# Flamingo-style decoder stack on Trainium2: in the first layer's prelude, ScalarE instead of VectorE takes the first block of each transposed pair out of PSUM

## The reference, cut to what matters

```python
def _rmsnorm(x, weight):
    var = jnp.mean(jnp.square(x), axis=-1, keepdims=True)
    return x * jax.lax.rsqrt(var + EPS) * weight
x = _rmsnorm(hidden_states, ln_weight)
h_q = (x @ w_q.T).reshape(b, lq, H, DH)
h_k = (key_value_states @ w_k.T).reshape(b, lk, H, DH)
h_v = (key_value_states @ w_v.T).reshape(b, lk, H, DH)
```

## Time and profile before

| | |
|---|---|
| median of 3 runs | 1596.53 us (1595.96 to 1597.42) |
| the profiled execution | 1596.18 us |
| its span in the trace | 1594.5 us |
| TensorE matmul, busy | 1556.7 us, 98% |
| TensorE weight load | 1278.7 us, 80% |
| VectorE | 984.2 us, 62% |
| ScalarE | 796.1 us, 50% |
| POOL | 484.2 us, 30% |
| mean granted TensorE clock | 0.999 |

### The profile page before, as it was taken

How to read it: one execution, slowest core, us unless ns; L and a number is a source line. 1 busy time by engine, 2 the same in 40 slices (tenths; PEclk the granted TensorE clock), 3 DMA queues, 4 the chain that set the end, 5 groups by cost and what they waited for, 6 DMA issues and landing times.

```text
span 1594.5 us, 26459 instructions
## 1 busy us (share of the span) xinstructions
PE 1556.7 (98%) x9066; PEld 1278.7 (80%) x9066; DVE 984.2 (62%) x2597; ACT 796.1 (50%) x2279; POOL 484.2 (30%) x350
## 2 busy tenths in 40 slices
PE   9999999999999999999999999999999999999987
PEld 7788888888888888888886888888898788766556
DVE  6762663635636446265476676767676767756677
ACT  5442443434424344244342476667677332288874
POOL 3131320312203213032112613232323543377651
PEclk9999999999999999999999999999999999999999
DMA  5110111101111111111234011020202613000001
GB/s 182 54 44 30 57 43 53 43 30 56 43 39 43 43 56 43 39 43 44 67 93 159 14 40 53 20 72 0 79 1 80 226 54 105 17 11 14 5 2 53
DMA packets 36597, 85.67 MB, mean 54 GB/s; under 512 B 5808, under 2 KB 18736, under 8 KB 34480
## 3 DMA queue, kind: packets, MB, share of 16 engines
q1 hardware_dynamic: 36528, 84.80, 16.2%
HBM read 82.69 MB, written 2.10 MB: 53 GB/s over the span
## 4 chain that ended last, share of the span: by engine, by line
PE 78%; DVE 9%; ACT 4%; issue 3%; DVEq 2%; POOL 1%; DMA 1%; POOLq 0%; SPq 0%; ACTq 0%
PE banks L1288 10%; PE banks L1233 10%; PE banks L1206 10%; PE banks L1214 10%; PE banks L1448 9%; PE banks L1561 4%; PE banks L1345 3%; PE banks L1328 3%; PE banks L1526 3%; PE banks L1335 2%; PE banks L1668 2%; PE banks L1675 1%; PE banks L1691 1%; PE banks L1474 1%; PE banks L1698 1%
## 5 line engine op out<-in xcount | busy, mean ns | idle before, releaser
L559 POOL TENSOR_TENSOR w_q<-w_raw_q,w_q 128x1792 fp32r<-128x1792 f32 x15 | 61.1, 4071 | 479.3 <-ACT w_q L796 479.3
L1288 PE MATMUL banks<-w_o,atT 128*128 128x512 f32 x720 | 181.0, 396 | 0.0
L1206 PE MATMUL banks<-cT,w_k 128*128 128x512 f32 x720 | 178.0, 396 | 0.0
L1233 PE MATMUL banks<-w_v,cT 128*128 128x512 f32 x768 | 176.6, 390 | 0.0
L1233 PEld LDWEIGHTS banks<-w_v,cT 128*128 128x128 f32 x768 | 143.9, 188 | 29.8
L1214 PE MATMUL banks<-xT,w_q 128*128 128x512 f32 x672 | 163.7, 394 | 0.7 <-ACT kT L786 0.7
L2004 DVE TENSOR_TENSOR sA<-banks,pbias 128x512 f32<-128x512 f32 x62 | 42.7, 690 | 186.6 <-PE banks L1328 185.8
L1206 PEld LDWEIGHTS banks<-cT,w_k 128*128 128x128 f32 x720 | 131.9, 188 | 25.5
L1288 PEld LDWEIGHTS banks<-w_o,atT 128*128 128x128 f32 x720 | 131.7, 188 | 25.6
L1214 PEld LDWEIGHTS banks<-xT,w_q 128*128 128x128 f32 x672 | 123.7, 188 | 26.1 <-ACT kT L786 1.2
L855 ACT ACTIVATE sA<-sA,nmA 128x128 f32<-128x128 f32 x248 | 96.4, 393 | 55.8 <-DVE nmA L2009 55.5
(11 more groups left out here) (298 smaller groups left out, 3403.4 us busy)
## 6 DMA issues: line engine op xcount, KB each, us to landing
wo_raw<-in_wo SPq DMA_DIRECT2D x16, 768.0 KB, 4.4
w_raw_v<-in_w0v SPq DMA_DIRECT2D x8, 1024.0 KB, 4.7
w_raw_q<-in_w0q SPq DMA_DIRECT2D x16, 512.0 KB, 3.3
w_raw_k<-in_w0k SPq DMA_DIRECT2D x15, 512.0 KB, 3.4
w_raw_o<-in_w0o SPq DMA_DIRECT2D x15, 512.0 KB, 3.3
cTp<-in_ctxT SPq DMA_DIRECT2D x12, 512.0 KB, 4.3
wq_raw<-in_wq SPq DMA_DIRECT2D x1, 3072.0 KB, 10.2
x_res<-in_x SPq DMA_DIRECT2D x4, 512.0 KB, 11.4
```

The costliest lines, as they stand in the source:

```text
L559: pool.tensor_tensor(w_part[slot][1][:], w_raw[slot][:], w_part[slot][0][:].bitcast(F32), ALU.subtract).then_inc(S(f"w{slot}_lo"), 1)
L1206: mm = pe.matmul(dst, wk_[l][:, c, h * P:(h + 1) * P], cT[r][:, c, half * HT:(half + 1) * HT], start=c == 0 and n == 0, stop=c == DC - 1 a ...
L1233: mm = pe.matmul(dst, cT[l][:, c, b * P:(b + 1) * P], wv_[r][:, c, :], start=n == 0, stop=n == 3 * DC - 1)
L1288: mm = pe.matmul(dst, at_at(l, p, b // 4 * 2 + h)[:, t], w[r][:, h, :], start=start and n == 0, stop=stop and n == 5)
```

## The change

ScalarE gets a new step, `rows_scale(k)`: four activation copies of 128x128 out of bank 4, each with one column of the norm's weight as its scale, into the half of `stage[k]` that VectorE filled before. It stands ahead of the value stores of blocks 2 to 5, ahead of `rows_high(k)`; the one of pair 3 waits for the first `x_split`, since it writes the buffer of pair 0. VectorE's `rows_sums(k)` now multiplies bank 5 alone and then waits for ScalarE's block (`xl_ready`) before the differences. TensorE's `turn_x` waits for `xl_ready` for bank 4 and for `xw_ready` for bank 5. On VectorE `rows_sums(2)` moves ahead of Q's low part, and `rows_sums(3)` ahead of `rows_low(1)`. ScalarE's wait for the small loads (`g_loaded`) moves ahead of the loop. What is computed stays the same.

```diff
             def rows_high(k):
                 t = slice(k * P, (k + 1) * P)
                 if k == NPAIR - 1:
-                    act.wait_ge(S("xw_ready"), 3 * k + 2)
+                    act.wait_ge(S("xw_ready"), 2 * k + 1)
                     act.activation(xT[0][:, 0:2, :, t], stage[k][:, 0:2], ACT.Copy).then_inc(S("x_prep"), 1)
-                    act.wait_ge(S("xw_ready"), 3 * k + 3)
+                    act.wait_ge(S("xw_ready"), 2 * k + 2)
                     act.activation(xT[0][:, 2:, :, t], stage[k][:, 2:], ACT.Copy).then_inc(S("x_prep"), 1)
                     return
-                act.wait_ge(S("xw_ready"), 3 * k + 3)
+                act.wait_ge(S("xw_ready"), 2 * k + 2)
                 act.activation(xT[0][:, :, :, t], stage[k][:], ACT.Copy).then_inc(S("x_prep"), 1)
+
+            def rows_scale(k):
+                act.wait_ge(S("xr_used"), 2 * k + 1)
+                for c in range(DC):
+                    e = act.activation(stage[k][:, 2 + c // 2, c % 2, :], bank(4)[:, c * P:(c + 1) * P], ACT.Copy,
+                                       scale=ln_w[:, c:c + 1])
+                e.then_inc(S("xl_ready"), 1)
...
+            act.wait_ge(S("g_loaded"), 64)
             for b in range(2, NB):
+                if b < 2 + NPAIR:
+                    if b == 2 + NPAIR - 1:
+                        act.wait_ge(S("x_split"), 1)
+                    rows_scale(b - 2)
                 store_v(b, bank(b % 2), K_UNITS + b + 1)
                 if b < 2 + NPAIR:
                     rows_high(b - 2)
                 if b == 2:
                     round_q(0)
-            act.wait_ge(S("g_loaded"), 64)
             act.activation(gates[:], gates[:], ACT.Tanh).then_inc(S("gates_ready"), 1)
...
                     pe.wait_ge(S("xr_ready"), 2 * k + j + 1)
-                    if k > 0:
-                        pe.wait_ge(S("xw_ready"), 3 * (k - 1) + j + 1)
+                    if k > 0 and j == 0:
+                        pe.wait_ge(S("xl_ready"), k)
+                    if k > 0 and j == 1:
+                        pe.wait_ge(S("xw_ready"), 2 * k - 1)
...
             def rows_sums(k):
                 x = stage[k]
-                for j in range(2):
-                    dve.wait_ge(S("xr_used"), 2 * k + j + 1)
-                    dve.tensor_tensor(x[:, 2 - 2 * j:4 - 2 * j].rearrange("p s c t -> p (s c) t"),
-                                      bank(4 + j).rearrange("p (c t) -> p c t", c=DC),
-                                      ln_w[:].unsqueeze(2).to_broadcast([P, DC, P]), ALU.mult).then_inc(S("xw_ready"), 1)
+                dve.wait_ge(S("xr_used"), 2 * k + 2)
+                dve.tensor_tensor(x[:, 0:2].rearrange("p s c t -> p (s c) t"), bank(5).rearrange("p (c t) -> p c t", c=DC),
+                                  ln_w[:].unsqueeze(2).to_broadcast([P, DC, P]), ALU.mult).then_inc(S("xw_ready"), 1)
+                dve.wait_ge(S("xl_ready"), k + 1)
                 dve.drain()
...
             rows_sums(1)
             rows_low(0)
+            rows_sums(2)
             dve.wait_ge(S("wq_hi"), 1)
             dve.tensor_tensor(w_part["q"][1][:], w_raw["q"][:], w_part["q"][0][:].bitcast(F32),
                               ALU.subtract).then_inc(S("wq_lo"), 1)
-            rows_sums(2)
+            rows_sums(3)
             rows_low(1)
-            rows_sums(3)
             rows_low(2)
```

## The result

The changed kernel takes 1600.32 us (median of 12 runs, 1598.85 to 1601.89), the kernel before 1596.24 us (12 runs, 1594.25 to 1597.76): ratio 1.0024, 95% interval 1.0015 to 1.0033, so slower: the medians are 4.1 us apart, and the interval reaches from 2.4 to 5.3 us. Measured again beside other kernels it gave 1.0026 (1.0016 to 1.0036). The forecast was 1600.8.

A forecast was written before the change was run, and what follows sets the result against it. TensorE, busy 98% of the span, bounds the kernel, with VectorE second in the prelude. +3.00 and +1.74 us, less late savings, give +4.30 at query unit 0: 1600.8 us, range 1598.5 to 1603.1.

The forecast's parts named there:

- The two causes: ScalarE's prelude order: first block behind the diagonals, +3.00 us; second behind round_q, +1.74 us more by pair 1.
- nothing behind query unit 0 gives the delay back: After the prelude: TensorE's work is a chain of products in unchanged order, so the +4.30 us stays whole.
- VectorE as the second bound: In the prelude: VectorE has no idle time from 26.65 to 52.19; its last split leaves query unit 0 0.2 us slack.
- A: In the prelude: ScalarE's order makes new TensorE waits, query unit 0 4.30 us later; 1600.8 us; chance 0.55.
- B: In TensorE's new 3.75 us wait before turn_x(2): clock falls, at most +3.2, taken as 1.7 us; 1602.5; chance 0.20.
- C: On ScalarE: scaled copies out of PSUM cost no more than plain ones; +2.6 us, 1599.1 us; chance 0.12.
- D: On ScalarE: scales start when their bank is full, the 2.15 us gap goes; 2.4 us gained, 1594.1; chance 0.10.

The follow-up runs named there:

- second trace of the changed kernel: The changed kernel run again with no edit, beside other kernels on one chip: 1599.90 us, ratio 1.0026.
- dve_order: The kernel before with only VectorE's new order (the change's last hunk), ScalarE doing nothing new: 1595.97 us, ratio 1.0002.
- filler_two: The changed kernel with idle TensorE products in both new waits, 5 after value unit 2 and 13 after unit 3: 1600.76 us, ratio 1.0028.
- act_order: The changed kernel with three of ScalarE's four scaled blocks, and the small-loads wait, moved in its program order: 1593.92 us, again 1595.16 us.
- first_only: The changed kernel with only the first scaled block moved, behind value store 1, ahead of the last four diagonals: 1596.00 us, ratio 1.0004.
- act_part: The changed kernel with VectorE's order of before, so ScalarE's copies alone: 1600.36 us, ratio 1.0031.
- the last two kernels: act_order and the changed kernel, each with VectorE's mask step moved from ahead of the query sums to among them: 1593.63 and 1599.58 us.

## Why the prediction was right, point by point

**Right, as forecast.** The three `turn_x` starts were forecast at 31.08, 39.37 and 44.17. The first two came at 31.04 and 39.60; the third came at 47.11, with the clock lost. In the second trace of the changed kernel, whose first statistics are 0.58 us earlier than in the kernel before, the last two stand at 38.87 and 43.49, that is 39.45 and 44.07 on the forecast's scale. The two causes (the first block behind POOL's power and the diagonals, the second behind `round_q`) were each shown by moving one block. That nothing behind query unit 0 gives the delay back was right to 0.4 us up to POOL's L600, once the collision of the mask step is set apart; the rest of the span varies by 3.2 us. VectorE as the second bound, with 0.2 us of slack, was right: `dve_order` gained nothing.

**The sum.** A's +4.30 us at query unit 0 was +3.94 with the clock kept (37.80 - 33.86). Four copies took 1.12 us and not 1.28: 362 ns each, against 386 for the diagonals, whose source lies in SBUF, and 277 for the plain copy out of PSUM. That brought each of the four blocks 0.16 to 0.18 us earlier. Against it, VectorE stood for 0.50 us within the weight sums (L1887, "issue"), which no step of mine had; 0.42 of it came through to the rounding of Q's weights. On the scale of the forecast, the second trace has the differences of the four pairs at 30.86, 39.41, 44.03 and 48.66 for 31.03, 39.32, 44.12 and 48.92, and query unit 0 at 54.95 for 55.31; the last 0.10 is the handover of the split to TensorE, where I took 0.15 and it was 0.05 (53.63 + 0.69 = 54.32, then 54.37). The collision of the mask step adds 1.0 us behind query unit 0. The prediction named no step of VectorE behind the last split, and so gave no price to their moving onto POOL's.

**The rivals.** B was at its place in the profiled execution: the clock fell in the second wait and the distance grew by 39.83 - 33.86 = 6.0 us, as B's middle gave. But `filler_two` shows that a kept clock leaves the median where it is. C fell (0.36 us, not 0.28). D fell for this change, and its mechanism was found right once ScalarE's order was mended: `act_order` starts its scales when their bank is full, and with the mask step moved it is faster than before beyond its interval. D's price, 2.4 us, was 1.7 in the distance and 0.7 to 2.4 in the medians.

**The margin.** The loss is 0.24%, near the 0.2% that counts as measurable, as A's +4.3 against 3.2 us had said. That the time came within 0.5 us of the forecast is in part luck. Up to POOL's L600 the two traces of the changed kernel are 4.8 us (clock kept in the second wait, mask step in collision) and 5.6 us (clock lost there) behind the kernel before, both more than the forecast's 4.3. I had 0.36 us too much in the prelude and had not seen 1.0 us behind it; the medians lie 4.1 and 3.5 us apart, within the spread.

**What stays open.** Where VectorE's 0.50 us of "issue" comes from: it is in every kernel here with ScalarE's blocks, at the second of the weight sums, and not in the two without them; nothing was tried on it. What decides whether a wait of some two us loses the clock: see below.

## What to carry to other kernels

Work moved to an engine with idle time starts not when its input is ready but when everything ahead of it in that engine's program is through, with whatever that waits for: write down, for the new step, what each instruction ahead of it waits on. That a gap in the bound engine closes is no gain by itself: it isn't worth its length if the engine that ends it has no slack of its own up to the next meeting point. And once a prelude is shortened, look at which pairs of instructions of VectorE and POOL now meet that didn't before.

## What the runs showed of the hardware that I had not expected

**VectorE and POOL hold each other up on SBUF.** VectorE instructions given out while a POOL subtraction ran ended 0.3 to 0.6 us after POOL's: 4.10 us for a 128x256 subtraction (0.42 alone), 2.89 us for the 128x1024 mask step (0.69 alone) in seven traces. It goes the other way as well. In `dve_order` POOL's key split was given out while VectorE's last split ran, and took 3.45 us in place of 2.40; it ended at 54.53, 2.25 us after VectorE's:

```profile
50.19 2.09 DVE L1935 TENSOR_TENSOR xT<-stage_q,xT 128x512 fp32r<-128x512 f32 x2
```

```profile
51.08 3.45 POOL L559 TENSOR_TENSOR w_k<-w_raw_k,w_k 128x1024 fp32r<-128x1024 f32 x1 [22.58 <-ACT w_k L779]
```

In the kernel before, the mask step (52.11 to 52.80) was over when POOL's split began (52.94), so nothing met there. But the same trace has the collision later, at POOL's split of Q's weights in pair after pair; I show the first:

```profile
73.56 0.69 DVE L2004 TENSOR_TENSOR sA<-banks,pbias 128x512 f32<-128x512 f32 x1 [1.07 <-PE banks L1328]
74.38 1.83 DVE L2009 CUSTOM_DVE_ANT_0 sA<-sA,madd 128x128 f32<-128x128 f32 x1
```

```profile
72.03 4.04 POOL L559 TENSOR_TENSOR w_q<-w_raw_q,w_q 128x1792 fp32r<-128x1792 f32 x1 [16.70 <-ACT w_q L796]
```

The instruction with both inputs in SBUF took 1.83 us in place of 0.29 and ended 0.14 us after POOL's. The one before it, with an input in PSUM (`banks`), kept its 0.69. The Trainium skill ("GPSIMD Engine Reference", Specifications) states that GpSimd's SBUF interfaces are shared with VectorE, with contention for instructions "in a 2-port perf mode or with two SBUF inputs". The traces agree for those with two inputs. Of those with one, the mask step was held up; the statistics of `x_res` (L1980), given out at 846.00 inside POOL's 845.61 to 848.15, were not (1.28 us for two, 678 ns for one in the median). For the mask step it would need the first clause; the traces don't show an instruction's mode.

**The length of a wait of some two us doesn't say whether the clock is kept.** Kept: 2.15 us in the kernel before. Lost: 1.84 us in the second trace of the changed kernel, 2.20 in `first_only`; in both the clock fell only when TensorE was busy again, 0.9 and 0.4 us after its return. Even 3.76 us in `act_part` left it at 1.00 until TensorE had been back for 1.2 us. What decides it was not tried. Once lost, it stayed at 0.50 for some 7 us in the first trace of the changed kernel, with TensorE busy for nearly all of it, and for some 3.4 us in the second.

**The spread of the runs goes with the clock, and hardly with the prelude.** The kernel before ran at mean clocks of 0.997 to 1.000; in 21 runs beside the last two kernels, those at 0.998 took 1596.5 us in the median (8 runs) and those at 0.999 took 1594.6 (8 runs). Behind the prelude, the granted clock of its trace is 0.97 from 1200 to 1250 us, that of the changed kernel's 0.97 from 1250 to 1300. Behind POOL's L600 alone, where all programs are the same, the fourteen traces differ by 3.2 us.
